# Queries of chunk 0 by halves, key rings cleared by ScalarE, and six more turned quarters taken by ScalarE

## The reference

```python
x = x + tanh(g_xattn[l]) * xattn(layernorm(x), ctx, ctx, ...)
x = x + tanh(g_ffn[l])   * ffn(layernorm(x), ...)
# cross-attention, 16 heads of width 8
q, k, v = split_heads(x @ wq + bq), split_heads(ctx @ wk + bk), split_heads(ctx @ wv + bv)
p = softmax(q @ k.T / sqrt(8) + mask)        # layer 0: p = p * group_prob afterwards
out = concat_heads(p @ v) @ wo + bo
# ffn, layer 0: 8 experts, top 2, capacity 1076 rows, gelu, gathered by slot
# ffn, layer 1: 8 experts, top 2, a * sigmoid(b), computed for all rows and weighted
```

## Time and profile before

| | |
|---|---|
| median of 3 runs | 934.35 us (934.09 to 935.02) |
| profiled execution | 936.31 us, its span 934.3 us |
| first maxima of layer 0 | 32.96 us |
| first maxima of layer 1 | 448.56 us |
| busy share of the span | PE 84%, DVE 74%, ACT 66%, POOL 58% |
| queue driven by hardware (q1) | 92.13 MB, 38.4% of 16 engines |

### The profile page before, as it was taken

One profiled execution on the slowest core, in us unless ns is written; L12 is line 12 of the kernel. 1 busy time (PEld: TensorE's weight loads), 2 busy tenths in 40 slices (PEclk: granted clock), 3 DMA queues, 4 the chain that ended last, 5 costly groups with the idle time before them and its releaser, 6 DMA issues.

```text
span 934.3 us, 20420 instructions
## 1 busy us (share of the span) xinstructions
PE 788.9 (84%) x6554; PEld 619.4 (66%) x6554; DVE 687.7 (74%) x1981; ACT 612.3 (66%) x2590; POOL 545.4 (58%) x786
## 2 busy tenths in 40 slices
PE   4698989888967399999678778788888889999997
PEld 1466666666744399998455546566656668888886
DVE  5798888987957434436599999899897675666665
ACT  2698889877842345444578888889996444444443
POOL 4556578887475301121556777765414867777775
PEclk9999999999975799999889999999998999999999
DMA  7998886466126643223454457356300000000000
GB/s 197 224 301 230 219 274 151 107 147 159 43 66 193 213 132 88 82 82 99 86 118 112 97 109 172 94 132 140 86 13 24 22 24 24 24 16 9 12 12 23
DMA packets 85138, 101.68 MB, mean 109 GB/s; under 512 B 8448, under 2 KB 70853, under 8 KB 84360
## 3 DMA queue, kind: packets, MB, share of 16 engines
q1 hardware_dynamic: 80936, 92.13, 38.4%
q0 software_dynamic: 4096, 8.25, 3.4%
HBM read 63.32 MB, written 45.99 MB: 117 GB/s over the span
## 4 chain that ended last, share of the span: by engine, by line
PE 40%; DVE 26%; ACT 14%; issue 9%; POOL 4%; another core or an unknown queue 3%; DMA 2%; SPq 1%; DVEq 0%; POOLq 0%; ACTq 0%
ACT exp L866 11%; PE psum L709 6%; DVE shift L1054 6%; PE psum L749 5%; PE psum L751 5%; PE psum L750 5%; DVE exp_T L1064 3%; DVE exp_T L1066 2%; DVE ln_stats L1036 2%; PE psum L592 2%; PE psum L697 2%; PE psum L579 2%; PE psum L698 2%; PE psum L699 2%
## 5 line engine op out<-in xcount | busy, mean ns | idle before, releaser
L866 ACT ACTIVATE exp<-psum,shift 128x120 f32<-128x120 f32 x1024 | 367.3, 443 | 77.3 <-DVE shift L1054 69.6
L866 ACT ACTIVATION_READ_ACCUMULATOR exp<-psum,shift 128x1 f32 x1024 | 276.2, 288 | 0.0
L579 PE MATMUL psum<-ident,exp 128*120 128x128 f32 x1024 | 163.4, 284 | 38.3 <-DVE exp_T L1066 21.8
L1054 DVE TENSOR_REDUCE shift<-psum 128x4 f32<-128x480 f32 x256 | 165.1, 646 | 29.1 <-PE psum L570 17.9
L1440 DVE SCALAR_TENSOR_TENSOR q_operand<-psum,comb,q_operand 128x256 f32<-128x256 f32 x256 | 111.5, 478 | 73.7 <-ACT q_operand L998 73.7
L1685 POOL TENSOR_TENSOR q_operand<-q_operand 128x512 f32<-128x512 f32 x95 | 125.3, 1318 | 58.1 <-DVE q_operand L1440 53.4
L579 PEld LDWEIGHTS psum<-ident,exp 128*120 128x120 f32 x1024 | 118.1, 141 | 59.6 <-DVE exp_T L1066 27.8
L998 ACT ACTIVATE q_operand<-psum 128x512 f32<-128x512 f32 x128 | 76.2, 599 | 114.6 <-PE psum L751 114.6
L1613 POOL DMA_INDIRECT got_rows<-scratch_y,slot_get x64 | 68.0, 1063 | 121.5 <-DMA scratch_y<-y_rows 104.7
L567 PE MATMUL psum<-neg_rows,const_bf 128*128 128x480 bf16 x256 | 98.2, 383 | 39.2 <-ACT exp L866 29.0
L570 PE MATMUL psum<-k_operand,q_operand 128*128 128x240 bf16 x512 | 97.1, 272 | 0.0
(11 more groups left out here) (177 smaller groups left out, 1670.4 us busy)
## 6 DMA issues: line engine op xcount, KB each, us to landing
k_operand<-scratch_k SPq DMA_DIRECT2D x32, 360.0 KB
q_operand<-scratch_q SPq DMA_DIRECT2D x30, 384.0 KB
scratch_q<-parts SPq DMA_DIRECT2D x15, 384.0 KB
scratch_k<-parts SPq DMA_DIRECT2D x14, 360.0 KB
scratch_xe<-in_zero_rows SPq DMA_DIRECT2D x8, 512.0 KB, 9.5
scratch_y<-in_zero_rows SPq DMA_DIRECT2D x8, 512.0 KB
scratch_q<-parts SPq DMA_DIRECT2D x15, 256.0 KB
scratch_k<-parts SPq DMA_DIRECT2D x14, 240.0 KB
```

The costliest lines, as they stand in the source:

```text
L579: ins = pe.transpose(ps[0:S2, T_BANKS[G % 2], u * S:(u + 1) * S], atts[l].expS[:, G % RING_E, u, :], ident[:, :])
L866: ins = act.activation(atts[l].expS[:, G % RING_E, u, :], ps[:, S_BANKS[G % 3], u * S2:(u + 1) * S2], ACT.Exp, bias=atts[l].shift[:, i % 2 ...
L1054: dve.tensor_reduce(atts[l].shift[:, i % 2, 4 * r:4 * r + 4], ps[:, S_BANKS[G % 3], 0:4 * S2].rearrange("p (h k) -> p h k", h=4), AX_X, AL ...
```

## The change

Queries of chunk 0 are written and read by halves of 256 tokens, that is batches 0 and 1, then 2 and 3. `first_out` writes the three outputs of one half, `first_in` reads it with two DMAs. The scores of rows 0 and 1 wait for the first half (`q0_in`), rows 2 and 3 for the second. SP's order is: first half out, `fetch_k(0)`, first half in, second half out, second half in. `part0(0, 1)` on ACT waits for both halves' outputs.

DVE splits the queries of chunk 0 ahead of `stat_rows(0, 1)`. The split of chunk 1's queries moves from before slot 0 into slot 1, `take_v(0)` into slot 2.

Rings 1 and 2 of `kop` are cleared by ACT, by a copy of one zero column broadcast over 3840 columns: ring 1 ahead of all else, ring 2 between `part0(1, 1)` and `take_turned(0, 1)`. POOL sets the zero column first of all.

`ALSO_TAKEN` becomes 4 to 15 (all rows of chunks 1 to 3), 17 and 19: ACT takes r = 1 of rows 4, 6, 8, 10, 12 and 14 of layer 1 as well.

```diff
@@ -220,7 +220,7 @@
-ALSO_TAKEN = range(CB + 1, 5 * CB, 2)
+ALSO_TAKEN = [*range(CB, 4 * CB), *range(4 * CB + 1, 5 * CB, 2)]
@@ -282,6 +282,7 @@
     half_c = sb(top, "minus_half", [128, CB])
+    zero_c = sb(top, "zero", [128, 1])
     xn = sb(top, "xn_rows", [S, 3, CB, D])
@@ -395,12 +396,12 @@
     ld_x, ld_first, ld_w, ld_rows = sem("ld_x"), sem("ld_first"), sem("ld_w"), sems("ld_rows", 3)
-    const, kop_zero, spread0 = sem("const"), sem("kop_zero"), sem("spread0")
+    const, zero_done, kop_zero, kop_zero_a, spread0 = sem("const"), sem("zero"), sem("kop_zero"), sem("kop_zero_a"), sem("spread0")
     spare_in = sem("spare_rows")
...
     ln_norm, ln_T, ln_Tout = sems("ln_norm", 2), sems("ln_T", 2), sems("ln_Tout", 2)
-    mm_q, q_proj, q_part, q_left, q_out, q_in = sem("mm_q"), sem("q_proj"), sem("q_part"), sem("q_left"), sem("q_out"), sems("q_in", RING)
+    mm_q, q_proj, q_part, q_left, q_out, q_in, q0_out, q0_in = sem("mm_q"), sem("q_proj"), sem("q_part"), sem("q_left"), sem("q_out"), sems("q_in", RING), sem("q0_out"), sem("q0_in")
     mm_k, k_proj, k_part, k_left, k_out, k_in = sem("mm_k"), sem("k_proj"), sem("k_part"), sem("k_left"), sem("k_out"), sems("k_in", RING)
@@ -561,6 +562,8 @@
                 on.wait_ge(h_in, 32)
+            elif C == 0 and b < CB // 2:
+                on.wait_ge(q0_in, 32)
             else:
@@ -835,6 +838,8 @@
                 on.wait_ge(h_out, 48)
+            if not k and C == 1:
+                on.wait_ge(q0_out, 48)
             act.copy(p[:, 0, at], f[:, at]).then_inc(h_part if h else part, 1)
@@ -925,11 +930,19 @@
+        def clear_ring(r):
+            flat = kop[:, r].rearrange("p a b c -> p (a b c)").bitcast(F32)
+            on.wait_ge(zero_done, 1)
+            act.copy(flat, zero_c[:].broadcast_to([128, PAIRS * CK])).then_inc(kop_zero_a, 1)
...
             if l == 0:
+                clear_ring(1)
                 for C in range(READY):
...
                     part0(1, C)
+                    if C == 1:
+                        clear_ring(2)
                     take_turned(0, C)
@@ -1281,6 +1294,11 @@
                 scale_bo1()
+            if l == 0 and s == 1:
+                split(0, 1)
+            if l == 0 and s == 2:
+                on.wait_ge(ld_w, 128)
+                take_v(0)
             if l == 1 and s == HALF1["q_left0"]:
@@ -1461,17 +1479,14 @@
         split(1, 0)
+        split(0, 0)
         stat_rows(0, 1, 0, 1)
-        split(0, 0)
         roots(0, 1)
...
             dve.tensor_scalar(bo[:, l, :], bo[:, l, :], tg_x[:, l:l + 1], None, ALU.mult).then_inc(bo_done, 1)
-        split(0, 1)
-        on.wait_ge(ld_w, 128)
-        take_v(0)
         attention(0)
@@ -1688,6 +1703,7 @@
+        pool.memset(zero_c[:], 0.0).then_inc(zero_done, 1)
         pool.memset(half_c[:], -0.5).then_inc(const, 1)
@@ -1696,8 +1712,6 @@
             add_bias(C)
-        clear_ring(1)
-        clear_ring(2)
         attention(0)
@@ -1753,6 +1767,21 @@
+        def first_out(second):
+            at = slice(second * CT // 2, (second + 1) * CT // 2)
+            for p, (slot, part, count) in enumerate(((5, 0, 1), (3, 0, 2), (0, 0, 3))):
+                on.wait_ge(*((q_part, p + 1) if p < 2 else (q_left, 2)))
+                sp.dma_start(q_dram[0][:, slot:slot + count, at], parts[:, 0, part:part + count, at]).then_inc(q_out if second else q0_out, 16)
+        def first_in(second):
+            at = slice(second * CT // 2, (second + 1) * CT // 2)
+            on.wait_ge(spare_in, 32)
+            on.wait_ge(*((q_out, 48) if second else (q0_out, 48)))
+            for i in range(2):
+                sp.dma_start(qop[HALF * i:HALF * i + SLOT_ROWS, 0, :, at],
+                             q_dram[0].rearrange("(t i d) s n -> i (d s) t n", i=2, d=DH)[i][:, :, at]).then_inc(q_in[0] if second else q0_in, 16)
@@ -1790,7 +1819,10 @@
                 on.wait_ge(key_out[(C - NCH - 2) % 3], 48 * ((C - NCH - 2) // 3 + 1))
-            on.wait_ge(kop_zero, r + 1)
+            if r == 0:
+                on.wait_ge(kop_zero, 1)
+            else:
+                on.wait_ge(kop_zero_a, r)
             for i in range(2):
@@ -1954,11 +1986,11 @@
             parts_out(1, 0, p)
-        parts_out(0, 0, 0)
+        first_out(0)
         fetch_k(0)
-        parts_out(0, 0, 1)
-        parts_out(0, 0, 2)
-        fetch_q(0)
+        first_in(0)
+        first_out(1)
+        first_in(1)
         load_group(0)
```

## The result

The changed kernel took 928.79 us in the median of 6 runs (927.73 to 936.41), the kernel before 934.22 beside it; the ratio is 0.9947 with a 95% interval of 0.9924 to 0.997, so 5.0 us less (2.8 to 7.1). The forecast was 930.1, that is 4.25 less. Its profile is of the slowest of the six executions, 936.41 us, so a second one was taken (`again`, 927.3 us), and both are read.

What follows compares the result with a forecast made beforehand. The prediction took the query fetch, then ScalarE, to bound layer 0's first slots, and DVE to be nearest its limit in layer 1. Start -3.65 and copies -0.6 gave -4.25, so 930.1 us, range 926.8 to 932.7.

Steps and rivals of the forecast that it cites:

- DVE's order: Start: chunk 0's split runs 13.75 to 15.6 us, statistics at 15.6 instead of 14.07; dependent chunk 1 work moves back 1.55.
- Halves: Start: first half of chunk 0's queries, fetched behind the keys from 18 us, lands at 25 instead of 31.9, no longer last.
- What is late next: Start: project_v and ScalarE's part 0 end at 26.8 us, scores 26.8, first exp 28.5; 5.15 us gained so far.
- What lay under the fetch: Layer 0's first slots: split and take_v, formerly hidden, cost 0.6 and 0.9, together 1.5; gain falls from 5.15 to 3.65.
- The clears: ScalarE's ring clears at the start: 3.3 to 4.4 us each, 3.9 taken; both covered, the second ending at 20.8 to 21.9.
- I charge nothing: Layer 0 after the start: queues lead by some 2 us, slots by 3.65; slack covers the difference, 0 to 2 kept as loss.
- the slack of 38.63: Layer 0, kernel before: chunk 2's rows were there without a wait at 38.63 us, where chunk 2's statistics begin.
- nothing has a fixed time: Behind chunk 1's queries, layer 0 and the experts were to shift as a block, keeping the start's lead.
- Rival A: Queues decide: chunk 2's rows or chunk 1's queries land only 2 us earlier, cutting the start's gain to 2; 931.7, chance 0.13.
- Layer 1: Six copies moved from DVE to ScalarE: rows 4, 6 and 12 zero, row 8 +0.6, rows 10 and 14 -0.6 each; sum -0.6.
- Rival C: Layer 1: DVE bounds it at all six places, so the copies give -3.6 us; 927.1 in total, chance 0.10.

Runs made afterwards that it cites:

- again: The changed kernel itself run once more, for a second profile and a closer ratio against the kernel before: 0.9958 (-3.9 us).
- whole: The changed kernel with chunk 0's queries written and fetched whole again, without the two waits for halves: 0.9951 of the kernel before (-4.6 us).
- hole_zero: The changed kernel with chunk 2's rows asked for ahead of the second half's fetch and scratch_xe zeroed from slot 34, not 16: 0.9939 of the kernel before.
- layer1_only: The kernel before with only the new ALSO_TAKEN, six layer 1 copies moved to ScalarE: ratio 0.9958 (-3.9 us).
- start_only: The changed kernel's start with ALSO_TAKEN as before, so layer 1 unchanged: ratio 1.0001 to the kernel before (+0.1 us).
- pad: The kernel before with the new ALSO_TAKEN, DVE given an unread maximum in place of each of the six copies: 1.002 (+1.9 us).

## Why the total was right, and the terms were not

1. DVE's order: right. Split at 13.65, statistics at 15.45. Chunk 1 was 0.9 late (take_turned's block at 21.64 against 20.75), not 1.55; GpSimd's first small operation, alone, took 0.23 us instead of 0.57.
2. Halves: right as a landing; the half fetch was issued at 18.03 and didn't end last. As a gain it was not needed here: `whole` does as well.
3. What is late next: right. Scores at 26.65 (26.8 forecast), first exp at 28.17 (28.5). ScalarE's part 0 stood 2.24 us, to 27.38, for the second half's outputs, a full microsecond later than I had it. That cost the exp nothing: part 0 was done at 28.00, and the exp then waited 0.17 for DVE's maxima.
4. What lay under the fetch: right in kind, and near in size as `hole_zero` shows (lead at slot 6 over `layer1_only` 3.64, over before 3.42, forecast 3.65). That it meets the forecast so closely is partly luck: the old starts differ by 1.9 at slot 6, and the wait for the group in slot 3, which I had held harmless, took 1.28.
5. The clears: 3.39 and 3.38 us, in the lower part of my 3.3 to 4.4. The second ended at 20.92, before the turned block. The estimate that stood beside it, from the Trainium skill (ScalarE: Activation LUTs), 3.4 us, agrees with both rows.
6. "I charge nothing": this step failed. Two waits that I had looked at or for took the whole lead. Chunk 2's rows landed no earlier than before, because SP issues them behind the second half's fetch, which waits for outputs until 27.33; I had given the queues a lead of 2 us, and for these rows it was none (36.73 against 36.68); I had not carried SP's own delay into the slack of 38.63, for which I had 1.5 us and which was 3.0. And behind slot 16 I had said that nothing has a fixed time; the zeroing has, by volume, and chunk 2's queries stand behind it, with PE's fall to the lower clock on top. Rival A named the mechanism and the first of the two loads, at a chance of 0.13 and a loss of 1.65; by `start_only` the loss was 3.65 (2.2 to 5.1). The measured term is 0 (1.4 less to 1.5 more), and with both waits mended -2.9 (-4.8 to -1.1).
7. Layer 1: mis-sized, -0.6 forecast, -3.9 (-5.4 to -2.4) measured. Place by place, the last three paid in the traces, as I had it for two of them; rows 4 and 6, which I had put at nothing, are among the three that cost. I had counted 0.6 a copy in one profile's chain, and that chain had only two of the six copies of DVE in it. By time the six together are worth 3.9 us, 0.65 a copy, about their length; what `pad` puts in their place, six times 0.64 us, cost 5.8 (3.6 to 8.0) by the two ratios. That more than the length comes back is not shown. Rival C, -3.6, was right in size at a chance of 0.10, though the traces don't show all six places paying. In the traces the two stretches give 1.7 us by their means (seven traces with the six copies, two without, all outside the third chip), and layer 1 up to the end of the kernel 2.3 to 4.8 in six of the seven; the seventh, the first of the changed kernel, is 0.9 to 1.4 longer than the two without, with a mean clock of 0.87 from slot 64 to 80, where most have 0.95. The two sets of three copies, -0.2 and -0.8, add up to less than the 3.9, but the difference of 2.9 us has an interval from -0.4 to 6.1, and they ran on another chip. So it is not shown that the sets are worth less apart than together.

So -3.65 and -0.6 became 0 and -3.9, and the sum stayed. That the total came out right was luck: two errors of over 3 us each cancelled, and only the kernels with one part each showed it.

## What to carry to other kernels

A lead won at the start lasts only as far as the next transfer in full queues: list the loads, the order in which the issuing engine reaches them, and the bulk writes that stand ahead, and compare each landing's slack with the lead. When an engine is busy over 90% in a stretch and others wait for it in turn, as DVE here, time taken off it can be worth its full length, whatever engine the chain names at that instant; price it by the stretch, and test it by padding. Take several traces of the same kernel before reading a lead of 1 or 2 us off two of them, and read the granted clock beside each length. Time each part of a change alone before crediting it.

## What the runs showed of the hardware

- A broadcast copy of 3840 columns on ScalarE took 3.38 us, GpSimd's memset of the same tile 3.30. DVE's bf16 cast took 4.86 us beside GpSimd's memsets and 0.43 at 29.33 with none beside it. No such cast fell beside ScalarE's clear; a subtraction of DVE over 480 columns that did, at 20.29, took 0.65; one over 512 columns with nothing beside it, at 13.65, took 0.69.
- After PE had stood 3.59 us for a landing (busy 0.46 of 2 us from 84 to 86), its granted clock fell from 1.00 to 0.50 and was 1.00 again from 90 on. After 1.5 us in `again` it did not fall. The same fall followed slot 4 of the changed start, where PE was busy 0.28 of 2 us from 34 to 36: 0.50 from 38 to 40.
- The kernel before took 934 to 935 us in its first measurement and on the first two chips of the experiments, and 917 on the third. The mean granted clock was 0.951 to 0.955 in the ten profiles of the former and 0.955 to 0.966 in the four of the latter. Part of the difference stands in one place: slots 92 to 124 of layer 0 took 57.5 us in each of the four traces of the third chip and 64.0 to 67.2 in the ten others. Why is open.
- From slot 40 to 64 of layer 1 eight traces agree within 0.06 us where ScalarE has the last three copies and DVE nothing in their place, and five without those copies spread over 3.6 us. What makes the spread was not tried and stays open.
